# Layer 2 experts of a two-layer recurrent block: when half an expert releases its activation, where the router's steps and the last products run, and how the result is stored

## The reference, cut to what matters

```python
X = X + out                                   # small attention of its own, projected
nx = _rmsnorm(X, g2)
xf = nx.reshape(-1, d)
logits = xf @ Wr.T + expert_bias              # 8 experts
rw = jax.nn.softmax(logits, axis=-1)
topw, topi = jax.lax.top_k(rw, TOP_K)         # TOP_K = 2
topw = jax.nn.softmax(topw, axis=-1)
combine = jnp.sum(jax.nn.one_hot(topi, NUM_EXPERTS, dtype=xf.dtype) * topw[..., None], axis=1)
shared = _swiglu(xf, sW1, sW2, sW3)
h = jax.nn.silu(jnp.einsum('td,efd->etf', xf, eW1)) * jnp.einsum('td,efd->etf', xf, eW3)
eo = jnp.einsum('etf,edf->etd', h, eW2)
specialist = jnp.einsum('te,etd->td', combine, eo)
g = X + shared + specialist                   # all widths are 128
x = x + s * _silu(g)
```

## Time and profile before

| What | Value |
|---|---|
| median of 3 runs | 723.9 us |
| profiled execution, its own time | 720.65 us |
| span of that execution | 718.9 us |
| PE busy (share of the span) | 623.3 us (87%) |
| DVE busy | 488.8 us (68%) |
| ACT busy | 353.0 us (49%) |
| POOL busy | 326.1 us (45%) |
| chain that ended last, by engine | PE 70%, DVE 15%, ACT 5%, issue 4% |
| granted PE clock, mean of the span | 0.944 of full speed |

### The profile page before, as it was taken

The page is one execution under the profiler, slowest core; times in us unless marked ns, Lnnn a source line. Parts: engine busy times, 40 slices in busy tenths (PEclk is TensorE's granted clock), DMA queues, the critical chain, the costliest instruction groups (busy, mean ns, idle before and its releaser), DMA issues.

```text
span 718.9 us, 12512 instructions
## 1 busy us (share of the span) xinstructions
PE 623.3 (87%) x4496; PEld 416.0 (58%) x4497; DVE 488.8 (68%) x1134; ACT 353.0 (49%) x713; POOL 326.1 (45%) x343
## 2 busy tenths in 40 slices
PE   3887689974975899888799999999999998798996
PEld 1465489953764366545455565555555553587885
DVE  7465245432958478767778788788888883678776
ACT  0542255531574455553267676576666666332222
POOL 6344300055404531541267778777787878032000
PEclk9997799997997899997699999999999999999999
DMA  9600102211000000000000000000000000000001
GB/s 304 269 1 31 44 16 70 62 48 26 1 0 1 1 2 3 2 2 2 0 1 1 1 1 0 2 0 1 1 1 1 1 0 1 1 1 15 1 16 29
DMA packets 16599, 17.31 MB, mean 24 GB/s; under 512 B 1696, under 2 KB 15008, under 8 KB 16160
## 3 DMA queue, kind: packets, MB, share of 16 engines
q1 hardware_dynamic: 15520, 14.48, 6.0%
q0 software_dynamic: 1024, 2.10, 1.0%
HBM read 11.34 MB, written 5.24 MB: 23 GB/s over the span
## 4 chain that ended last, share of the span: by engine, by line
PE 70%; DVE 15%; ACT 5%; issue 4%; another core or an unknown queue 2%; POOL 1%; DMA 1%; SPq 0%; DVEq 0%; POOLq 0%
PE ps L1870 12%; PE ps L1860 9%; PE ps L1850 8%; PE ps L1609 5%; PE ps L1999 4%; PE ps L1592 3%; PE ps L1656 3%; DVE region L1007 2%; PE ps L1765 2%; PE ps L1646 2%; PE ps L1781 2%; PE ps L1988 2%; PE ps L1990 2%; PE ps L1989 2%
## 5 line engine op out<-in xcount | busy, mean ns | idle before, releaser
L1007 DVE TENSOR_REDUCE region<-ps 128x1 f32<-128x512 f32 x256 | 161.5, 683 | 45.1 <-PE ps L1850 44.5
L1393 ACT ACTIVATE region<-ps 128x512 f32<-128x512 f32 x256 | 137.0, 600 | 60.0 <-PE ps L1860 60.0
L695 POOL TENSOR_TENSOR region<-region 128x512 f32<-128x512 f32 x80 | 109.0, 1364 | 53.1 <-ACT region L1393 49.5
L1860 PE MATMUL ps<-qmr,kr 98*128 98x512 f32 x256 | 112.1, 442 | 2.6 <-ACT region L1393 1.8
L1850 PE MATMUL ps<-kr,qmr 96*128 96x512 f32 x256 | 107.1, 427 | 7.4 <-DVE region L1007 7.2
L1877 PE MATMUL ps<-region,ones 128*32 128x512 f32 x192 | 92.4, 603 | 2.7 <-DVE region L1024 2.7
L1870 PE MATMUL ps<-region 128*32 128x512 f32 x512 | 91.8, 599 | 0.0
L700 POOL TENSOR_TENSOR region<-region 128x512 f32<-128x512 f32 x64 | 82.0, 1281 | 11.9 <-ACT region L1393 8.0
L1860 PEld LDWEIGHTS ps<-qmr,kr 98*128 98x128 f32 x256 | 49.0, 192 | 53.8 <-issue 27.2
L1609 PE MATMUL ps<-region 128*128 128x128 f32 x272 | 43.2, 311 | 25.4 <-ACT region L1251 17.7
L1850 PEld LDWEIGHTS ps<-kr,qmr 96*128 96x128 f32 x256 | 50.7, 200 | 23.1 <-DVE region L1007 16.1
(11 more groups left out here) (280 smaller groups left out, 1201.1 us busy)
## 6 DMA issues: line engine op xcount, KB each, us to landing
region<-in_w SPq DMA_DIRECT2D x2, 2048.0 KB, 12.9
slots_in<-zeros SPq DMA_DIRECT2D x1, 1536.0 KB, 9.1
region<-slots_in SPq DMA_DIRECT2D x6, 256.0 KB, 2.8
slots_out<-og SPq DMA_DIRECT2D x6, 256.0 KB, 2.4
e<-in_e SPq DMA_DIRECT2D x1, 1152.0 KB, 15.7
x<-in_x SPq DMA_DIRECT2D x4, 256.0 KB, 4.1
out<-y SPq DMA_DIRECT2D x4, 256.0 KB, 2.3
e<-in_e SPq DMA_DIRECT2D x1, 576.0 KB, 17.2
```

The source lines that it names most:

```text
L695: ins = pool.tensor_tensor(o, held(tiles[0]), held(tiles[1]), ALU.add)
L1007: dve.tensor_reduce(mxp[:, u // HM, u % HM:u % HM + 1], bank(b), AX.X, ALU.max).then_inc(mx_read, 1)
L1393: act.activation(pm[:, t // 2, t % 2 * HM * P:(t % 2 + 1) * HM * P], bank(SCORE_BANKS[n % 3]), ACT.Exp, scale=SCM).then_inc(p_whole, 1)
L1860: pe.matmul(bank(SCORE_BANKS[n % 3]), kr[0:M_ROWS, t * P:(t + 1) * P], qr[0:M_ROWS, parity, :], start=True, stop=True).then_inc(st_filled, 1)
```

## The change

1. **Half release.** PE counts the first half's last matmul on a new semaphore `h1_filled`. ACT's silu waits for that; DVE's product waits for silu and for `h13_filled` (second half).
2. **Router in three batches.** Tiles 0 to 7 (64 columns) are done in shared tiles 14 and 15; group 2 (32 columns) and group 3 (32 columns) in the expert stage, their exponents by POOL. The functions are cut to steps of one to three operations, one step behind each expert.
3. **Preparation of group 3** is spread: omT behind hidden of expert 2, mo behind 4, nxT in chunk 1 at expert 1, lg in chunk 1 at expert 3; DVE's statistics in two steps; ACT's copies moved accordingly.
4. **Products.** The `finish` of chunks 0 to 2 and of the first half of chunk 3 goes from DVE to POOL; DVE keeps the second half of chunk 3. `acc_ready` goes; ACT waits for `e_read` itself. ACT's last silu is cut in two.
5. **Table.** ACT loads the silu table ahead of `sums(NT - 1)`.
6. **Store.** The last chunk is stored as two halves, DVE's half first.

The old bodies of `first_place`, of POOL's power steps and of DVE's `finish` are printed above with the kernel and left out here.

```diff
@@ -60,7 +60,7 @@
         (13, 9): ("omT", 2), (14, 2): ("mo", 2), (15, 5): ("nxT", 2), (15, 9): ("lg", 2)}
-LAST_PREP = {1: ("omT", 3), 3: ("mo", 3), 7: ("nxT", 3), 8: ("lg", 3)}
+LAST_PREP = {(0, 2): ("omT", 3), (0, 4): ("mo", 3), (1, 1): ("nxT", 3), (1, 3): ("lg", 3)}
 MAX_START = 9
@@ -342,6 +342,14 @@
+        halves = [slice(NT - TG, NT - TG // 2), slice(NT - TG // 2, NT)]
+        def added_by(tile):
+            chunk, t = (tile - 1) // TG, (tile - 1) % TG
+            return (chunk * ES + ES - 1) * TG + t + 1
         s_x = [sem(f"s_x{g}") for g in range(NG)]
@@ -518,10 +526,14 @@
             rows_out = out.rearrange("(t p) d -> p t d", p=P)
-            for j in range(NCH):
+            for j in range(NCH - 1):
                 sp.wait_ge(fin_ready, j + 1)
                 sp.dma_start(rows_out[:, j * q_:(j + 1) * q_, :], y[:, j * q_:(j + 1) * q_, :]).then_inc(s_out, 16)
-            sp.wait_ge(s_out, 16 * NCH)
+            sp.wait_ge(last_ready, 1)
+            sp.dma_start(rows_out[:, halves[1], :], y[:, halves[1], :]).then_inc(s_out, 16)
+            sp.wait_ge(fin_ready, NCH)
+            sp.dma_start(rows_out[:, halves[0], :], y[:, halves[0], :]).then_inc(s_out, 16)
+            sp.wait_ge(s_out, 16 * (NCH + 1))
@@ -716,16 +728,36 @@
             pool.memset(euler[:, :, :], math.e).then_inc(euler_ready, 1)
+            def router_exponents(r, n):
+                pool.wait_ge(rx_ready, n)
+                pool.tensor_tensor(rw[:, r, :], euler[:, :, :], lg1[:, r, :], ALU.pow).then_inc(rpow_ready, 1)
+            def weight_exponents(r, n):
+                pool.wait_ge(rx_ready, n)
+                pool.tensor_tensor(w2nd[:, r], euler[:, 0, 0:TG], w2nd[:, r], ALU.pow).then_inc(rpow_ready, 1)
+            pool.wait_ge(euler_ready, 1)
+            router_exponents(each_group[2], 3)
             low_rows(1)
...
             low_rows(3)
...
+            router_exponents(each_group[3], 4)
+            weight_exponents(each_group[2], 5)
+            def finish(n, some):
+                pool.wait_ge(g1_ready, n + 1)
+                pool.tensor_tensor(y[:, some, :], y[:, some, :], s0[:, some, :], ALU.mult).then_inc(prod_ready, 1)
+                pool.wait_ge(prod_ready, n + 1)
+                pool.tensor_tensor(y[:, some, :], y[:, some, :], x[:, some, :], ALU.add).then_inc(fin_ready, 1)
+            finish(0, each_group[0])
+            finish(1, each_group[1])
+            weight_exponents(each_group[3], 6)
+            finish(2, each_group[2])
+            finish(3, halves[0])
@@ -1060,9 +1092,15 @@
-            def spread1(g):
+            def row_stats(g):
                 dve.wait_ge(x2_ready, g + 1)
-                variances(4, g, xn)
+                for t in range(TG * g, TG * (g + 1)):
+                    link.mark(dve.bn_stats(stats[:, t, :], xn[:, t, :]))
+            def row_spread(g):
+                link.wait()
+                for t in range(TG * g, TG * (g + 1)):
+                    dve.bn_aggr(mv[:, t, :], stats[:, t, :]).then_inc(var_ready[4], 1)
@@ -1072,39 +1110,45 @@
-            def router_differences(r, n):
+            def router_differences(r):
                 dve.wait_ge(lg_ready, r.stop // TG)
...
-            def router_places(r, exponents, n):
+            def shares(r, exponents, n):
                 dve.wait_ge(exponents, n)
...
                 link(dve.tensor_tensor(rw[:, r, :], rw[:, r, :], wide(mrow, r), ALU.mult))
-                first_place(oh1, first_w, r)
+            def largest(oh, best, r):
+                link(dve.tensor_reduce(best[:, r], rw[:, r, :], AX.X, ALU.max))
+                link(dve.tensor_tensor(oh[:, r, :], rw[:, r, :], wide(best, r), ALU.is_equal))
+            def first_place(oh, r):
+                link(dve.tensor_tensor(oh[:, r, :], oh[:, r, :], down_e[:, r, :], ALU.mult))
+                link(dve.tensor_reduce(mrow[:, r], oh[:, r, :], AX.X, ALU.max))
+                link(dve.tensor_tensor(oh[:, r, :], down_e[:, r, :], wide(mrow, r), ALU.is_equal))
+            def without_first(r):
                 link(dve.scalar_tensor_tensor(out=rw[:, r, :], in0=oh1[:, r, :], scalar=-2.0, in1=rw[:, r, :], op0=ALU.mult, op1=ALU.add))
-                first_place(oh2, second_w, r)
+            def weight_difference(r):
                 dve.tensor_tensor(w2nd[:, r], second_w[:, r], first_w[:, r], ALU.subtract).then_inc(rx_ready, 1)
...
-            def router_weights(r, exponents, n):
+            def both_weights(r, exponents, n):
                 dve.wait_ge(exponents, n)
...
                 link(dve.tensor_tensor(w2nd[:, r], w2nd[:, r], w1st[:, r], ALU.mult))
+            def combined(r):
                 link.mark(dve.tensor_tensor(ctmp[:, r, :], oh1[:, r, :], wide(w1st, r), ALU.mult))
...
-            early_rows, last_rows = slice(0, NT - TG), each_group[NG - 1]
+            early_rows = slice(0, NT - 2 * TG)
@@ -1124,22 +1168,34 @@
                     if t == 9 and i in (6, 10, 14):
-                        spread1((i - 6) // 4)
+                        row_stats((i - 6) // 4)
+                        row_spread((i - 6) // 4)
+                    if t == 9 and i == NT - 2:
+                        router_differences(early_rows)
+                    if t == 9 and i == NT - 1:
+                        shares(early_rows, rexp_ready, 1)
+                        largest(oh1, first_w, early_rows)
+                        first_place(oh1, early_rows)
+                        without_first(early_rows)
                     if t == 10 and i == NT - 1:
                         logits1(2)
-                        router_differences(early_rows, 0)
+                        largest(oh2, second_w, early_rows)
+                        first_place(oh2, early_rows)
                     if t == 12 and i == NT - 1:
-                        router_places(early_rows, rexp_ready, 1)
+                        weight_difference(early_rows)
+                        router_differences(each_group[2])
                     if t == OUT_SLOT and not first:
...
             last_sum(NT - 1)
-            router_weights(early_rows, rexp_ready, 2)
+            both_weights(early_rows, rexp_ready, 2)
+            combined(early_rows)
...
                 dve.wait_ge(sg_ready, n_ + 1)
+                dve.wait_ge(h13_filled, n_ + 1)
                 if n_ >= 2:
@@ -1156,13 +1212,11 @@
...
+            def finish(some):
+                dve.wait_ge(g1_ready, NCH + 1)
+                link(dve.tensor_tensor(y[:, some, :], y[:, some, :], s0[:, some, :], ALU.mult))
+                dve.tensor_tensor(y[:, some, :], y[:, some, :], x[:, some, :], ALU.add).then_inc(last_ready, 1)
@@ -1176,19 +1230,50 @@
                         residual1(NG - 1)
-                        spread1(NG - 1)
-                    if j == 0 and e == ES:
+                    if j == 0 and e == 5:
+                        row_stats(NG - 1)
+                    if j == 0 and e == 6:
+                        row_spread(NG - 1)
+                    if j == 0 and e == 7:
+                        shares(each_group[2], rpow_ready, 1)
+                    if j == 0 and e == 8:
+                        largest(oh1, first_w, each_group[2])
+                    if j == 1 and e == 0:
+                        first_place(oh1, each_group[2])
+                    if j == 1 and e == 1:
+                        without_first(each_group[2])
+                    if j == 1 and e == 2:
+                        largest(oh2, second_w, each_group[2])
+                    if j == 1 and e == 3:
+                        first_place(oh2, each_group[2])
+                    if j == 1 and e == 4:
                         logits1(NG - 1)
-                        router_differences(last_rows, 2)
+                        router_differences(each_group[3])
                     if j == 1 and e == 5:
-                        router_places(last_rows, rpow_ready, 1)
+                        weight_difference(each_group[2])
                     if j == 1 and e == 8:
-                        router_weights(last_rows, rpow_ready, 2)
-                    if j >= 1 and e == FINISH + 1:
-                        finish(j - 1)
-                dve.wait_ge(e_read, (j + 1) * ES * (CH // P))
-                dve.sem_inc(acc_ready, 1)
-            finish(NCH - 1)
+                        both_weights(each_group[2], rpow_ready, 3)
+                    if j == 2 and e == 0:
+                        combined(each_group[2])
+                    if j == 2 and e == 1:
+                        shares(each_group[3], rpow_ready, 2)
+                    if j == 2 and e == 2:
+                        largest(oh1, first_w, each_group[3])
+                    if j == 2 and e == 3:
+                        first_place(oh1, each_group[3])
+                    if j == 2 and e == 4:
+                        without_first(each_group[3])
+                    if j == 2 and e == 5:
+                        largest(oh2, second_w, each_group[3])
+                    if j == 2 and e == 6:
```

(56 more changed lines are left out.)

14 lines of the change are left out of this document (removed).

## The result

| | before | after |
|---|---|---|
| median of 4 runs each | 723.24 us (719.57 to 726.54) | 713.19 us (710.18 to 714.62) |
| ratio of the runs | | 0.9867, 95% interval 0.9818 to 0.9915 |
| profiled execution, its own time | 720.65 us | 712.10 us |
| its span | 718.9 us | 710.4 us |
| hidden(0) to the end of the last project | 95.9 us | 87.9 us |

The kernel is 10 us faster by the medians (the interval of the ratio leaves 6 to 13); forecast were 12.0, with a time of 711.9. The two profiled spans differ by 8.5 us. The stage of the experts gave 8.1 us. The start, for which 3.0 were forecast, gave 0.7 in this execution. In the table that is the last line, measured from the four transposes of `turn_maxima(15)`, behind which the last shared tile runs the same way in all kernels here up to the logits, apart from the clock; I call it tile 15.

What follows compares the result with a forecast made beforehand. PE was taken to bound the expert stage, with holes, and DVE its start. Gains of 13.1 us less 1.0 for collisions made 12.1, say 12.0: 723.9 - 12.0 = 711.9 us, range 707.5 to 718.0.

Steps and rivals of the forecast that it cites:

- Chunk sums: Expert stage: of 10.8 us of holes beyond 36 experts and group 3's PE work, 10.1 go; collisions cost 1.0.
- Burst: Chunk 1: 14 linked router operations stop PE 2.5 us, half clock adds 1.7; cutting them up gains 4.2 us.
- Group 3: Preparing group 3 in chunk 0: spreading it removes PE's wait at omT and smaller holes, 1.9 us.
- Half release: Silu starts after three of six hidden passes: 2.5 us gained at chunk ends, 0.8 in first rounds.
- Start: Start of the expert stage: fewer DVE router operations behind the logits bring hidden(0) to 613.96, 3.0 us gained.
- 0.7 for hidden(0) at full clock: Start of the expert stage: hidden(0) and its turn at full clock gain another 0.7 us.
- The signs: Changed profile: hidden(0) near 614, chunk starts 20.5 to 22.3 us apart, chunk-end holes under 0.1; wrong if 1 us steps delay PE.
- The power and the port: Rival at the stage's start: POOL's group 2 power locks DVE's port, last_sum waits, 8 us back, 719.9; chance 0.13.
- Products to POOL: Expert stage: small two-operand DVE steps meet POOL's products and wait, 1.0 us lost, bounds 0 and 4.
- table: Silu table load of 1.28 us, put under PE's last sums before the expert stage, stays at no cost.
- end: After the last project: POOL and DVE take turns at two-operand halves; taken as 0, bounds 0.9 gained, 0.5 lost.
- Clock as the slower case: Rival in chunks 1 and 2: small PE stops keep the clock low; 730 us with 9 such experts; chance 0.04.

Runs made afterwards that it cites:

- d4: Changed kernel with both halves of the last chunk on DVE and group 2's first router step behind expert 3 of chunk 0, not 7: 691.28 us, ratio 0.9833.
- d2: The kernel before with the half release alone added: 700.33 us, ratio 0.9954 to the kernel before.
- c1: The changed kernel run again without any edit: 694.14 us, ratio 0.9848 to the kernel before.
- c3: Changed kernel with group 3's seven router steps of chunk 2 all put behind expert 1: 695.03 us, ratio 0.9845 to the kernel before.
- c2: Changed kernel with the half release alone undone: 695.23 us, ratio 0.9845 to the kernel before.
- f2: Changed kernel without the early load of silu's table: 695.13 us, ratio 0.9838 to the kernel before.
- d1: The kernel before run again without any edit: ratio 1.0013 to the kernel before.
- d3: Changed kernel with both halves of the last chunk on DVE, stored in order: 693.29 us, ratio 0.9848 to the kernel before.

## Why the prediction was right, point by point

- **Chunk sums.** Leftover holes in the stage were forecast at 1.7 us (10.8 less 10.1, and 1.0 of collisions); they are 2.8 (87.9 less 82.1 and 3.0). The mechanism and the places are right, the size is 1 us off: one collision, with `low_rows(2)`, was not on my list, and moving the step away from it (d4) gives 1.1 us back. I had looked for POOL's products beside the small steps and not for the low rows whose time the change had moved.
- **Burst.** Forecast 4.2 gone with the half clock. Chunk 1 went from 25.8 to 22.1, that is by 3.7, though it now also holds 1.3 us of group 3's turn and logits (my estimate), and its share of the half release is in it too; from d2 to c1, which both have the half release, it is 2.5, or 3.8 with the 1.3. c3 shows the price of a burst in another place. The trace has 15 operations in the burst, not the 14 I counted; their 3.3 us are read rightly.
- **Group 3.** Forecast 1.9. No run takes it alone. From d2 to d4, which has no collision left in chunk 0, chunk 0 goes from 25.8 to 22.5 us; less the 1.3 that moved to chunk 1 that is 2.0, an estimate near the forecast.
- **Half release.** Forecast 3.3, measured 2.6 by undoing it. At a chunk's end the hole is 0.16, not 0.06 (in the trace two projects of 0.89 take 1.94 from 681.68 to 683.62). The cover of 1.5 us behind it was forecast. c3's burst of 3.3 cost 1.5, which makes it 1.8, and d2's left a hole of 2.07, which makes it 1.2: it depends on what DVE did just before.
- **Start.** Forecast 3.0: right in executions without the dip (3.2 from the turn; 23.4 in c1, c2 and f2), by the forecast's own chain of four waits for POOL's sums. The 0.7 for hidden(0) at full clock lies in chunk 0 and was not measured alone; in the kernel before with full clock there (d1) chunk 0 is 0.3 us shorter. The step that failed is a silent one: that the clock before hidden(0) would be what it was in the one trace I had. With the dip it is 1.2, and the dip is the more frequent case here.
- **The number.** The profiled span fell by 8.5 us, not 12.1: the start is 2.3 short, the stage 1.0, the end gave 0.2, and 0.5 was lost ahead of the turn of tile 15. The profiled execution was forecast at 708.7 us and took 712.10. That the median came within 1.3 us of 711.9 is partly luck: I took it as 3.25 us above the profiled execution, as before, and it was 1.1 above.
- **The signs.** hidden(0) near 614, and chunk starts at most 22.3 us apart, failed in the first profile (616.69, and 23.6 for chunk 0); c1 meets the first by its tile of 23.4 us, d4 comes near the second with 22.5. The hole at a chunk's end, 0.16, is over the 0.1 that was said. And one sign of being wrong was met at one place: a small step of 1.08 us (L1122) with PE stopped for 1.09 behind it.
- **The power and the port.** Rival refuted: last_sum starts 1.4 us into the power and lasts 0.69 (in c1 0.3 us into it, 0.68). The Trainium skill's rule (SBUF — State Buffer, "SBUF: two separate sides") that whoever starts first has the shared pair for the whole instruction holds for POOL's products and sums in every trace here (in all 266 cases where a VectorE operation with two SBUF operands started inside one, it ended no earlier than POOL's), and does not hold for the power, with 4 or 32 columns.
- **Products to POOL, table, end.** Neutral (0.25), 0.2 and 0.2 us: each inside its bounds. The end was taken at 0 because of the turns at the port. They are there, but cost only 0.2 us beside DVE alone (1.87 and 1.68 us for the four operations); the rest of d3's 0.8 is mostly the issue of the second store.
- **Clock as the slower case.** No stretch below full clock from 617 us to the last project. In the expert stages of the 14 traces the clock was full behind every hole up to 1.42 us and fell behind those of 2.07 and 2.29. This is no rule: in tile 15 it fell behind 1.09 and 0.28, and stayed full behind 2.49 in d2.

## What to carry to other kernels

Work that is cut into steps and put behind another engine's rounds costs next to nothing while each step is shorter than that engine's cover. Releasing the first half of a result early is worth its time where little other work covers the next engines (2.6 us here, at ends and beginnings of chunks); how much cover it adds for such steps depends on what stands in front of them (0.2 us from the kernel before to d2). Before moving a small two-operand VectorE step, look for GpSimd's products at the same moment: the step waits for all of one, however small it is. And when a chain is shortened, look at what was waiting in its shade: a disturbance that used to cost 0.5 us now costs 2.5, and one trace does not show how often it comes.

## What the runs showed of the hardware that I had not expected

The granted clock fell in the last shared tile in some executions and not in others of the same program, behind PE holes equal to 0.02 us (about 1.09 and 0.28 us), to 0.50 for 3.4 us each time, and a pass of PE's sums then took 0.86 instead of 0.43 us. A power of 32 columns keeps GpSimd busy for 5.44 us, and VectorE's additions with two SBUF operands run inside it at their usual 0.69 us, while those that meet a GpSimd product or sum of 512 columns (1.28 us) end only with it.
